# Last attention of a four-stage kernel: transposed scores and value sums at the head of TensorE's step

## What is computed

```python
q = (layernorm(x, ln_q_g, ln_q_b) @ Wq + bq).reshape(b, c, HEAD, HD).transpose(0, 2, 1, 3)
kv = (layernorm(x, ln_kv_g, ln_kv_b) @ Wkv + bkv).reshape(b, c, 2, HEAD, HD)
k, v = kv[:, :, 0].transpose(0, 2, 1, 3), kv[:, :, 1].transpose(0, 2, 1, 3)
q, k = apply_rotary(q * scale, x), apply_rotary(k * scale, x)
qn, kn = layernorm(q, ln_h_g, ln_h_b), layernorm(k, ln_h_g, ln_h_b)
logits = jnp.einsum('bhqd,bhkd->bhqk', qn, kn) / jnp.sqrt(jnp.float32(HD))
att = jax.nn.softmax(logits, axis=-1)
a = jnp.einsum('bhqk,bhkd->bhqd', att, v).transpose(0, 2, 1, 3).reshape(b, c, d)
return a @ Wo + bo
```

## Time and profile before

| | |
|---|---|
| median of 3 runs | 2774.77 us (2765.41 to 2776.35) |
| the profiled execution | 2782.3 us, of which span 2780.3 us |
| mean granted TensorE clock | 0.923 of full speed |
| busy share of the span | PE 84%, PEld 56%, DVE 59%, ACT 46%, POOL 49% |
| the last attention | from 1920 to 2366 us of the span, 16% of it |
| of it, steps with first scores and exponentials | from 2017 to 2317 us |

### The profile page before, as it was taken

How to read it: one execution, slowest core, us unless ns; L and a number is a source line. 1 busy time by engine, 2 the same in 40 slices (tenths; PEclk the granted TensorE clock), 3 DMA queues, 4 the chain that set the end, 5 groups by cost and what they waited for, 6 DMA issues and landing times. The chain is left out here.

```text
span 2780.3 us, 41037 instructions
## 1 busy us (share of the span) xinstructions
PE 2342.3 (84%) x12100; PEld 1559.3 (56%) x12100; DVE 1649.0 (59%) x5313; ACT 1274.5 (46%) x3678; POOL 1358.1 (49%) x1301
## 2 busy tenths in 40 slices
PE   6999999994899999999998499963577887599991
PEld 5888888882455555555554456531333343466661
DVE  7667676665766766766774533327566753653334
ACT  3444444443556656656666244421166564143331
POOL 2444454441555555555554178862634310138885
PEclk9999999997899999999999599985799998699996
DMA  5000000002000000000001545550000000515554
GB/s 167 16 15 1 15 15 15 16 4 87 1 1 1 1 1 1 1 1 1 1 1 32 219 81 87 86 117 23 0 1 1 1 1 1 198 35 86 87 85 112
DMA packets 72818, 112.26 MB, mean 40 GB/s; under 512 B 11504, under 2 KB 59632, under 8 KB 72240
## 3 DMA queue, kind: packets, MB, share of 16 engines
q0 software_dynamic: 30336, 42.73, 9.3%
q1 hardware_dynamic: 38080, 63.15, 6.5%
q10 hardware_dynamic: 4224, 4.19, 0.4%
HBM read 80.69 MB, written 36.32 MB: 42 GB/s over the span
## 5 line engine op out<-in xcount | busy, mean ns | idle before, releaser
L1059 POOL TENSOR_TENSOR b_sm<-b_sm,b_rden 128x128 f32<-128x128 f32 (+3 forms) x512 | 355.7, 722 | 357.4 <-DVE b_rden L1012 357.4
L952 ACT ACTIVATE b_sm<-b_sm,b_mn 128x128 f32<-128x128 f32 (+3 forms) x512 | 285.1, 569 | 23.0 <-DVE b_mn L1004 22.0
L943 ACT ACTIVATE b_pt<-b_t 128x128 f32<-128x128 f32 (+3 forms) x512 | 196.1, 440 | 144.9 <-PE b_t L883 144.5
L1004 DVE CUSTOM_DVE_ANT_0 b_sm<-b_f,maskB 128x128 f32<-128x128 f32 (+3 forms) x512 | 233.5, 489 | 3.3 <-issue 2.2
L873 PE MATMUL b_f<-b_k,b_q 64*128 64x128 f32 (+3 forms) x1024 | 209.9, 486 | 29.1 <-DVE b_prod L993 14.7
L993 DVE SCALAR_TENSOR_TENSOR b_prod<-b_f,b_sin 32x512 f32<-32x512 f32 x320 | 219.9, 687 | 4.3
L1428 POOL DMA_INDIRECT XN<-rows,m_slots x158 | 158.1, 1001 | 94.0 <-issue 47.5
L2080 DVE TENSOR_REDUCE c_nm<-c_first 128x2 f32<-128x1024 f32 x128 | 155.1, 1219 | 82.2 <-PE c_first L1835 82.2
L1980 ACT ACTIVATE c_pt<-c_second 128x512 f32<-128x512 f32 x256 | 139.2, 598 | 123.8 <-PE c_second L1848 123.6
L883 PE MATMUL b_t<-ident,b_sm 128*128 128x128 f32 x1280 | 194.6, 283 | 0.9 <-ACT b_pt L943 0.8
L409 POOL TENSOR_TENSOR a_q<-a_prod 128x512 f32<-128x512 f32 x64 | 81.8, 1278 | 228.8 <-DVE a_prod L355 228.8
(11 more groups left out here) (283 smaller groups left out, 5393.4 us busy)
## 6 DMA issues: line engine op xcount, KB each, us to landing
WM<-in_m_w_dram SPq DMA_DIRECT2D x4, 3072.0 KB, 17.5
WM<-in_m_w_dram SPq DMA_DIRECT2D x4, 2432.0 KB, 14.0
acc<-in_zeros_dram SPq DMA_DIRECT2D x3, 2176.0 KB, 16.2
n_part<-acc SPq DMA_DIRECT2D x12, 512.0 KB, 7.8
a_wa<-in_a_wa_dram SPq DMA_DIRECT2D x8, 512.0 KB, 4.5
b_w<-in_b_w_dram SPq DMA_DIRECT2D x1, 3072.0 KB, 9.9
XN<-rows,m_slots POOLq DMA_INDIRECT x158, 2.8
X<-in_x_dram SPq DMA_DIRECT2D x4, 512.0 KB, 5.7
```

The costliest lines, as they stand in the source:

```text
L943: act.activation(pt[:, M % 2, head, 0:t + 1, t * P:(t + 1) * P], back_bank(("t", S, head))[:, 0:keys(t)].rearrange("p (k n) -> p k n", n=P ...
L952: act.activation(sm[:, s, 0:keys(t)], sm[:, s, 0:keys(t)], ACT.Exp, scale=-1.0, bias=mn[:, s:s + 1], accum_out=den[:, s:s + 1]).then_inc(s ...
L1004: dve.tensor_tensor_reduce(sm[:, s, 0:keys(t)], front_bank(("s", S, head))[:, 0:keys(t)], mask[:, SEQ - keys(t):SEQ], 1.0, -3 * NEG, ALU.a ...
L1059: pool.tensor_tensor(sm[:, s, 0:keys(t)], sm[:, s, 0:keys(t)], rden[:, s:s + 1].to_broadcast([P, keys(t)]), ALU.mult).then_inc(s_pn, 1)
```

## The change

On TensorE, in the loop over s in `attention2`, the calls of `scores_t(s - 14)` and `values` move from the end of the step to its head. All waits move with the calls; the calls themselves, the constants SECOND and LAG, the lists `pairs` and `singles`, and the programs of the other engines stay as they were.

```diff
                 for s in range(FIRST_STEP, LAST_STEP):
+                    g = s - SECOND
+                    if 0 <= g < NP:
+                        scores_t(g)
+                    m = g - LAG
+                    if 0 <= m < NP and m % 2 == 1:
+                        values(m // 2)
                     if turned_again(s) is not None:
                         pe.wait_ge(s_nl, turned_again(s) + 1)
                         turn_q("again", turned_again(s), s_tr2)
@@
                     for half in range(2):
                         if batch_at(s, OUT_AT + half) is not None:
                             out(batch_at(s, OUT_AT + half) * 2 + half)
-                    g = s - SECOND
-                    if 0 <= g < NP:
-                        scores_t(g)
-                    m = g - LAG
-                    if 0 <= m < NP and m % 2 == 1:
-                        values(m // 2)
```

## The result

The changed kernel takes 2786.99 us (median of 19 runs, 2774.8 to 2801.9), the kernel before 2774.84 us on the same chips (19 runs). The ratio is 1.0044, with a 95% interval of 1.0025 to 1.0063: 12.2 us slower (7 to 17.5), less than the 13.9 us that were called no change. The forecast was 2775 in a range of 2762 to 2794.

What follows compares the result with a forecast made beforehand. No engine was taken as the bound everywhere; who waits for whom in each step decides. Terms -1.8 - 5.7 - 4.4 + 10.5 + 0.7 + 1.2 = +0.5 us on 2774.77 gave 2775, range 2762 to 2794.

Steps and rivals of the forecast that it cites:

- The sequence: TensorE's loop: same order of calls round the loop, but `scores_t` runs one step ahead while ScalarE's program order stays.
- (a): Step 3 of 8: ScalarE waits for q's second turn behind `scores_t` and `values`; 4.7 us to the next `scores_t`, not 1.8.
- (b): Step 0 of 8: exponentials queue behind ScalarE's copy of the maximum and start 1.0 to 1.1 us late.
- the light group of 18.55 us: Eight steps of the last batch, with no next batch to prepare: 18.55 us against 15.05, +3.5 us each.
- The last group: Last eight steps of the light batch: output matmuls hide most of the loss, +0.7 us.
- the clock as a rival: Light batch: more idle time lowers TensorE's granted clock, 0.6 us a step, 19 us, total 2794; chance 0.08.
- Heavy batches: The two batches that prepare the next one beside the attention: -5.7 us for the first, -4.4 for the second.
- The first stretch: From 2017 to 2068.61 us, where scores of both kinds first meet: -1.8 us, mostly by the root.
- (d): Gains: earlier exponentials free ScalarE's copies and root; the keys' turns lose 1.95 us waits, V's projection most of 2.73.
- (c): `values` shares its interval with odd steps' other TensorE work, leaving less slack under the exponentials: +1.2 us a heavy batch.
- The sentence that hid it: VectorE: `copy_o` loses 18.0 us of waits for `values`, which now delays first scores by 1.0 us; counted as nothing.
- The rival that was faster: Waits for copies and root go, with (a) and (b) hidden: -15 to -20 us, 2758; chance 0.06.

Runs made afterwards that it cites:

- e1_exps_first: Changed kernel with ScalarE's exponentials moved ahead of the copies of the maximum and of the second turn of q: 2766.03 us, ratio 0.9954.
- e4_refill: Changed kernel with the last batch's first scores written four and three times over at steps 0 and 3 of each group: 2783.12 us, ratio 1.0016.
- e7_again: Changed kernel with only `scores_t` at the head of the step and `values` left at its end, timed a second time: 2749.08 us, ratio 0.9921.
- e5_exps_before_copy: Changed kernel with ScalarE's exponentials moved ahead of the copy of the second turn of q, but behind `max_high`: 2780.64 us, ratio 1.0003.

## Why the prediction was right, and where it was not

The class and the range held: 2787 is in 2762 to 2794, and 12.2 us is less than 13.9, though not by much. The forecast itself, 2775, is 12 us too low.

- The sequence. That S2 runs one step ahead while ScalarE's order stays is what the timeline shows, and `e1_exps_first` gives 21 us back by that order alone.
- (a) and (b), the light group of 18.55 us. The places are right, and the size is nearly, at the higher clock: 18.2 in `e4_refill` (ScalarE's idle time before the copy of the second turn is 2.6 us there, and 4.65 in after, where about 1.5 was expected). **This is the term that was mis-sized**: +11.2 us for the light batch, measured +20.7. The walk used durations at the higher clock for a loop that TensorE now spends waiting; the clock fell to 0.77 to 0.84, and 7.9 us of the batch hang on it. The last group is a smaller miss: 0.7 us were counted, and it grew by 1.9 (16.1 to 18.0) at clock 1.00. I had the clock as a rival, as a case that excludes the forecast (2794, 0.08). It came together with the forecast, at less than half its price of 19 us. The mark written down for it, a clock row of the light batch below 1.00, is what was found, and by the prediction's own last sentence it says that this part was wrong.
- Heavy batches, 88.7 for the second: 89.2 and 87.8 (92.0 and 92.3 in two more executions, at clock 0.94), and -6.8 against -5.7 for the first. Right in the sum, and partly by luck: the transposed scores alone take 12 us off the first (94.4 to 82.6), and V gives 5.2 back, where the walk had smaller amounts of both.
- The first stretch, -1.8: -1.9. Right.
- (d), keys and root. The waits of 1.95 at i = 27 fell to 0.77, those at i = 29 to nothing; the one of 2.73 to 1.02, not to 0.2. Smaller than said, but in the walk's sum.
- (c), V's place, was the wrong step, though the total does not show it. I priced it by the X that V shares an interval with: +1.2 us for a heavy batch. For a light group its 1.0 us stands in step (a) alone. By `e7_again` against after it is 5.2 us in the first heavy batch and 5.2 to 6.6 in the second, and by light groups of 16.1 against 18.2 (`e4_refill`) 2.1 us each. V shares its interval with the same X in both kernels, so that X is not what it costs.
- The sentence that hid it is "V now delays S1 and its maximum by the 1.0 us instead, so I count this as nothing". VectorE's `copy_o` waits for V once in eight steps, and nobody waits for it soon. For S1 VectorE waits in every step, and ScalarE behind it; for the turn ScalarE waits, and S1 stands behind the turn on TensorE. The 18.0 us of the earlier trace rows were idle time that cost nothing, and the exchange was not even.

So two halves of opposite sign were walked as one: S2 at the head gains 22 to 33 us, V at the head costs 19 us alone and 38 beside the other half (there, a part of it by the clock of the light batch). The rival that was faster (2758, 0.06) had the first half right, and underrated it.

What stays open: how much of the 38 us is the turn and how much S1, since no run puts V between the two; why V behind the turn is worth 2.1 us a light group at the full clock, where its expectation had about 1; and why some tails run at 0.63 to 0.75 and others above 0.9.

## What to carry to other kernels

In a step of an engine that works in order, put first what another engine waits for, and last what nobody waits for soon; one matmul group of 1.0 us, in front of S1 and the turns instead of behind them (64 such groups in this kernel), cost 38 us. When a change moves two calls, walk each half alone, because their sum can hide a gain that is twice as large. And a stream that is shifted by a step must be followed into its consumer's own program order; where that makes TensorE wait more, add what the clock may do, from rows of the same kernel at a lower clock.

## What was not expected of the hardware

TensorE's granted clock fell from 1.00 to 0.77 to 0.84 in a loop that never stops, where TensorE waits 0.75 to 2.06 us at a time, and stayed at 1.00 when more matmuls cut these waits to 0.94 to 1.37 us (`e4_refill`). One such wait does not bring it down: the third light group of `e5_exps_before_copy` has one of 2.06 us at 1.00. A turn of eight transposes is 1.09 us at the higher level (2.4 GHz) and 1.97 at the lower (1.2 GHz). The tail took from 38.3 us (`e1_exps_first`) to 50.6 us (`e4_refill`) with nearly the same instructions, and for one kernel 39.3 and 46.4 us (at 0.96 and 0.71).
